# Cross attention: sums of probabilities, their spreading and the value weights' products, each moved behind the value products of their step

## The reference, cut to what matters

```python
kvx = einsum('bsi,oi->bso', cond, w_kv_x)      # cond: 16 x 1500 x 256, kept in float32
kx, vx = split(kvx, 2)                         # 8 groups of 128 each
kx = _ln(kx, kxln_w, kxln_b)
p = softmax(einsum('bsghd,btgd->bghst', qx, kx) / sqrt(128))
xout = einsum('bghst,btgd->bsghd', p, vx)      # 16 heads, 56 queries, 1500 keys
catq = _div_clamp_fp8(cat([core, xout]), proj_smooth)
```

## Time and profile before

| | us |
|---|---|
| median of 3 runs (lowest, highest) | 2561.54 (2557.67, 2563.57) |
| the profiled execution, its own time | 2560.54 |
| its span, first to last instruction | 2558.5 |
| cross attention, from first scores to last `ca` | 1123.8 to 2310.8 |
| TensorE busy over the span | 2341.7 (92%) |
| mean granted clock of TensorE | 0.95 of full |

### The profile page before, as it was taken

The page is one execution under the profiler, slowest core; times in us unless marked ns, Lnnn a source line. Parts: engine busy times, 40 slices in busy tenths (PEclk is TensorE's granted clock), DMA queues, the critical chain, the costliest instruction groups (busy, mean ns, idle before and its releaser), DMA issues. The chain is left out here.

```text
span 2558.5 us, 38343 instructions
## 1 busy us (share of the span) xinstructions
PE 2341.7 (92%) x12603; PEld 2045.3 (80%) x12603; DVE 2019.6 (79%) x3952; ACT 1088.3 (43%) x1849; POOL 919.4 (36%) x640
## 2 busy tenths in 40 slices
PE   7999999999984788859999999999999999986797
PEld 6777777779983666658888888988888888976797
DVE  8999987877757887848888888888888888871487
ACT  1000001108855666614544554455545454554332
POOL 5455100200012344424545544555455444570000
PEclk9999999999996888879999999999999999997899
DMA  9667623517624010042222212222222112106211
GB/s 389 263 266 274 240 99 145 191 66 255 220 98 144 37 44 36 29 135 77 84 74 79 69 46 80 83 80 69 74 83 71 63 57 83 61 4 162 56 55 39
DMA packets 143384, 286.66 MB, mean 112 GB/s; under 512 B 26033, under 2 KB 114178, under 8 KB 139202
## 3 DMA queue, kind: packets, MB, share of 16 engines
q1 hardware_dynamic: 137266, 265.40, 30.0%
q0 software_dynamic: 6032, 20.20, 2.1%
HBM read 203.91 MB, written 81.66 MB: 112 GB/s over the span
## 5 line engine op out<-in xcount | busy, mean ns | idle before, releaser
L1697 POOL TENSOR_TENSOR s_acc<-s_acc,s_sx 125x896 f32<-125x896 f32 x128 | 275.8, 2154 | 261.3 <-DVE s_mxh L1941 114.6
L572 DVE BATCH_NORM_STATS2 s_st<-ps 125x6 f32<-125x128 f32 x1536 | 318.7, 280 | 55.6 <-PE ps L444 49.1
L1896 DVE TENSOR_TENSOR s_sx<-ps,keep_krs 125x896 f32<-125x896 f32 x192 | 208.9, 1088 | 167.3 <-PE ps L1807 164.1
L1761 ACT ACTIVATE s_sx<-s_sx 125x896 f32<-125x896 f32 x192 | 183.2, 954 | 352.8 <-DVE s_sx L1914 352.8
L1858 PE MATMUL ps<-s_p_hi,s_cn_hi 125*128 125x448 f32 x768 | 304.1, 396 | 6.6 <-DVE s_p_lo L1920 6.2
L1920 DVE TENSOR_TENSOR s_p_lo<-s_sx,s_p_hi 125x896 fp32r<-125x896 f32 x192 | 290.7, 1514 | 3.1 <-ACT s_p_hi L1766 3.1
L1807 PE MATMUL ps<-s_qc_hi,s_ct_hi 128*125 128x448 f32 x768 | 288.3, 375 | 1.3 <-DVE s_qc_lo L1879 1.3
L1858 PE MATMUL ps<-s_p_lo,s_cn_hi 125*128 125x448 f32 x768 | 285.1, 371 | 0.0
L1858 PE MATMUL ps<-s_p_hi,s_cn_lo 125*128 125x448 f32 x768 | 285.1, 371 | 0.0
L1807 PE MATMUL ps<-s_qc_lo,s_ct_hi 128*125 128x448 f32 x768 | 282.5, 368 | 0.0
L1807 PE MATMUL ps<-s_qc_hi,s_ct_lo 128*125 128x448 f32 x768 | 282.3, 368 | 0.0
(11 more groups left out here) (378 smaller groups left out, 5646.1 us busy)
## 6 DMA issues: line engine op xcount, KB each, us to landing
l_ahead<-in_ctxt SPq DMA_DIRECT2D x16, 1500.0 KB, 8.6
s_ct_hi<-ct_hi SPq DMA_DIRECT2D x48, 500.0 KB, 4.2
s_ct_lo<-ct_lo SPq DMA_DIRECT2D x48, 500.0 KB, 4.9
s_cn_raw<-in_ctx SPq DMA_DIRECT2D x48, 500.0 KB
l_raw<-in_ctxt SPq DMA_DIRECT2D x15, 1500.0 KB, 10.4
l_raw<-in_w SPq DMA_DIRECT2D x16, 1024.0 KB, 5.4
ct_hi<-l_hi SPq DMA_DIRECT2D x8, 1500.0 KB, 12.1
ct_lo<-l_lo SPq DMA_DIRECT2D x8, 1500.0 KB, 16.3
```

The costliest lines, as they stand in the source:

```text
L572: ins = dve.bn_stats(st[:, G * t + g, :], kx[0:TT, t % NB, g // 4, DH * (g % 4):DH * (g % 4) + DH])
L1697: pool.tensor_tensor(a, a, p[:, PR * w.pt:PR * w.pt + PR, :], ALU.add).then_inc(s["acc_ready"], 1)
L1761: act.activation(p, p, ACT.Exp).then_inc(s["exp_ready"], 1)
L1896: dve.tensor_tensor(by_group(sx[w.h][:, tiles, :]), by_group(sc[st % 2]), krs_b[:, tiles, HG * w.h:HG * w.h + HG].unsqueeze(3).to_broadcas ...
```

## The change

In the cross attention alone, nothing is added or removed; eight edits move work within the steps.

- TensorE: the value products of a step come right after its scores and what belongs to the maxima, ahead of the sums, the spread and the value weights' products.
- ScalarE: in step 3 the copy to `ut` comes first and `rdiag` no longer follows it there but begins step 4; `rsc` begins step 5 and not step 4.
- VectorE: the reciprocal `r4` goes from behind L1896 to the end of step 3; `ca` goes from step 5 to step 0 of the next unit, behind `p_lo`.
- The tail has one more call, for `ca` of the last unit.

```diff
@@ steps_of
             body(B)
+            act(B + 1, 0)
             act(B + 1, 3)
@@ ScalarE
-                    if w.i == 3 and w.two_back:
+                    if w.i == 4 and w.two_back:
                         act.wait_ge(s["r4_ready"], w.u - 1)
...
                         ins.then_inc(s["rdiag_ready"], 1)
...
-                    if w.i == 4 and w.two_back:
+                    if w.i == 5 and w.two_back:
                         act.wait_ge(s["rb_ready"], w.u - 1)
@@ TensorE: this block is moved up, from behind the value weights' products
+                    if w.has_v:
+                        pe.wait_ge(s["lo_ready"], w.v + 1)
+                        if w.vt == 0 and not (static(w.vu) and w.vu < 1):
+                            pe.wait_ge(s["ut_read"], w.vu)
...
+                        for j in range(PR):
+                            t = PR * w.vt + j
...
+                        mm.then_inc(s["pv_ready"], 1)
                     if w.i == 3 and w.two_back:
                         pe.wait_ge(s["acc_ready"], NPR * (w.u - 1))
@@ VectorE
-                    if w.i == NPR - 1 and w.two_back:
-                        dve.wait_ge(s["rb_read"], w.u - 1)
-                        dve.wait_ge(s["v_ready"], w.u - 1)
+                    if w.i == 0 and w.three_back:
+                        dve.wait_ge(s["rb_read"], w.u - 2)
+                        dve.wait_ge(s["v_ready"], w.u - 2)
                         dve.tensor_tensor(ca[:, :], misc[:, 0:QH], rsc[:, :], ALU.mult).then_inc(s["v_read"], 1)
...
+                    if w.i == 3 and w.two_back:
+                        dve.wait_ge(s["sum_ready"], w.u - 1)
...
+                        dve.reciprocal(r4[:, :], sums).then_inc(s["r4_ready"], 1)
```

More of the change, by code:

```diff
@@ L1821, in run @@
                         pe.matmul(mb, ones_r[:, :], diag[:, :, :], start=True, stop=True).then_inc(s["mb_ready"], 1)
+                    if w.has_v:
+                        pe.wait_ge(s["lo_ready"], w.v + 1)
+                        if w.vt == 0 and not (static(w.vu) and w.vu < 1):
+                            pe.wait_ge(s["ut_read"], w.vu)
+                        if w.vh == 0 and PR * w.vt % CHT == 0:
+                            vb = b + (st - V_LAG) // STEPS
+                            pe.wait_ge(s["cn_lo_ready"], NCH * vb + PR * w.vt // CHT + 1)
+                        for j in range(PR):
+                            t = PR * w.vt + j
+                            for k in range(K2):
+                                c = 0
+                                for x, pp in ((cn_hi, (p_hi, p_lo)), (cn_lo, (p_hi,))):
+                                    for y in pp:
+                                        mm = pe.matmul(pv[:, k, :], x[:, t, k * P:k * P + P], y[w.vr][:, j, :],
+                                                       start=(t == 0 and c == 0), stop=(t == NT - 1 and c == 2))
+                                        c += 1
+                        mm.then_inc(s["pv_ready"], 1)
                     if w.i == 3 and w.two_back:
@@ L1844, in run @@
                         mm.then_inc(s["v_ready"], 1)
-                    if w.has_v:
-                        pe.wait_ge(s["lo_ready"], w.v + 1)
-                        if w.vt == 0 and not (static(w.vu) and w.vu < 1):
-                            pe.wait_ge(s["ut_read"], w.vu)
-                        if w.vh == 0 and PR * w.vt % CHT == 0:
-                            vb = b + (st - V_LAG) // STEPS
-                            pe.wait_ge(s["cn_lo_ready"], NCH * vb + PR * w.vt // CHT + 1)
-                        for j in range(PR):
-                            t = PR * w.vt + j
-                            for k in range(K2):
-                                c = 0
-                                for x, pp in ((cn_hi, (p_hi, p_lo)), (cn_lo, (p_hi,))):
-                                    for y in pp:
-                                        mm = pe.matmul(pv[:, k, :], x[:, t, k * P:k * P + P], y[w.vr][:, j, :],
-                                                       start=(t == 0 and c == 0), stop=(t == NT - 1 and c == 2))
-                                        c += 1
-                        mm.then_inc(s["pv_ready"], 1)
                     if w.i == 1 and w.new and w.next:
@@ L1904, in run @@
                         qc_split(w.u + 1, 1 - w.h, 0)
-                    if w.i == 3 and w.two_back:
-                        dve.wait_ge(s["sum_ready"], w.u - 1)
-                        if not (static(b) and w.u < 3):
-                            dve.wait_ge(s["rdiag_ready"], w.u - 2)
-                        dve.reciprocal(r4[:, :], sums).then_inc(s["r4_ready"], 1)
                     if w.has_p:
```

10 lines of the change are left out of this document (6 added, 4 removed).

## The result

The changed kernel took 2526.36 us (median of 4 runs, 2524.0 to 2527.13), the kernel before 2559.88 on the same chip (4 runs, 2557.67 to 2563.57): a ratio of 0.9866, 95% interval 0.9849 to 0.9883. Run twice more, it gave 2526.03 (0.9867, 0.9851 to 0.9884) and 2526.53 (0.987, 0.9848 to 0.9891). Forecast were 2530 and a range of 2522 to 2545. The profiled execution took 2525.84 with a span of 2523.8 us, against 2560.54 and 2558.5.

A forecast was written before the change was run, and what follows sets the result against it. TensorE's queue was taken to bound the kernel, standing still mainly at the sums. Terms 21.2 - 3.5 + 6.3 + 6.4 = 30.4 us off the profiled 2560.5 gave 2530, range 2522 to 2545.

The forecast's parts named there:

- The waits at the sums: Steady units, TensorE: value products first remove waits of 1.18 us in 14 odd and 0.36 in 13 even units, 21.2 us.
- The clock: Four of 14 odd units, steps 3 and 4: slow-clock stretches of 1.57 us each all go, 6.3 us.
- The new wait for `p_lo`: Step 5 of 14 odd units: value products wait 0.25 us for `p_lo` of step 4, 3.5 us back.
- The lower bound of 0: Smallest size of the step 5 `p_lo` wait: GpSimd's chain follows fully and `p_lo` is not blocked.
- the 24.0 of the terms: Steady units: 21.2 us for the sums' waits, minus 3.5 for `p_lo`, plus 6.3 for the clock.
- The tail: After the last scores: GpSimd's chain 3.3 us sooner, sums to spread 3.05 shorter; 6.4 us, at least 3, at most 8.
- The edits priced at nothing: Moved `ut`, reciprocal, `rdiag`, `rsc`, value weights' products and `ca` cost nothing in steady units; `ca` covered by 0.4 us.
- VectorE and GpSimd did not become the pace: Rival, odd units: their chain does not tighten and the 1.18 us wait returns at step 5 or spread; 2543 to 2549, chance 0.12.
- The clock did not stay slow: Rival, odd units: the clock dips stay because thin sums stay; 2536, chance 0.10.
- The collisions: Rival, steps 4 and 5 of odd units: two more blocked `p_lo` per pair of units cost 46 us; 2576, chance 0.05.
- It does not do what it says: Rival, at the sums: a second wait stood just behind `qc_lo`; 2555 to 2561, chance 0.04.
- Odd units of 35.5: Sign, scores to scores: odd units take 35.5 us instead of 36.4; wrong if still 36 or more.

The follow-up runs named there:

- The filler of 0.62 us: The changed kernel with 0.62 us of extra VectorE work ahead of `p_lo` in step 4 of odd units; 2528.46 us, ratio 0.9884.
- the run with the earlier add: The changed kernel, but GpSimd's first add of step 3 no longer waits for that step's running maximum; 2593.76 us, ratio 1.0144.

## Why the prediction was right, and where its terms were off

**The waits at the sums: 21.2 predicted, about 23.5 measured.** This term was right. Odd units without a slow clock went from 36.4 to 35.1, 1.3 and not 1.18; even ones from 35.6 to 35.2, 0.4 and not 0.36. The difference is the sums themselves: they held TensorE 0.80 us behind a wait and hold it 0.72 now (1653.48 - 1652.76). It is 0.80 to 0.83 in the steady units of the other runs in which they wait, too. 27 x 0.08 = 2.2 us that the term had left out.

**The clock: 6.3 predicted, about 8.1 measured.** All four slow stretches (units 5, 11, 19 and 27) went, as taken. A slow odd unit cost 1.5 to 1.6 us, as worked out, and in three of the four cases the even unit behind it another 0.6 to 0.7 (36.2 or 36.3 in place of 35.6), which the two windows of the earlier trace rows end too early to show. That second part is a collision and not the clock. The kernel before in step 1 behind the first slow unit, on TensorE, VectorE and GpSimd:

```profile
1324.86 0.47 PE L1858 MATMUL ps<-s_p_hi,s_cn_hi 125*128 125x448 f32 x1 [0.40 <-DVE s_p_lo L1920]
...
1321.50 3.31 DVE L1920 TENSOR_TENSOR s_p_lo<-s_sx,s_p_hi 125x896 fp32r<-125x896 f32 x1
...
1321.44 2.42 POOL L1705 TENSOR_TENSOR s_cn_lo<-s_cn_raw,s_cn_hi 125x1024 fp32r<-125x1024 f32 x1
```

and in the same step of an even unit that follows no slow one:

```profile
1394.67 1.08 DVE L1920 TENSOR_TENSOR s_p_lo<-s_sx,s_p_hi 125x896 fp32r<-125x896 f32 x1
...
1394.70 3.31 POOL L1705 TENSOR_TENSOR s_cn_lo<-s_cn_raw,s_cn_hi 125x1024 fp32r<-125x1024 f32 x1
```

`p_lo` is 0.06 us behind `cn_lo` in the one and 0.03 ahead in the other, and takes 3.31 or 1.08. It is 3.31 behind three of the four slow units, and TensorE waits for it there.

**The new wait for `p_lo`: 3.5 predicted, none measured.** This is the step that failed. The prediction moved GpSimd's start by the right amount: its first add is released by the running maximum (217.2 us in 27 waits) and starts 25.7 us into the unit where it had started 26.2 into it. But the prediction left VectorE's `p_lo` where it was, and the change moves that further. VectorE's scaling of the scores in step 4 had waited 1.11 us for them, and that wait is gone. `p_lo` starts 27.65 us into the unit and no longer 28.92, and so 0.17 ahead of `cn_lo`. The filler of 0.62 us put the order back, and the wait with it. The lower bound of 0, "`p_lo` not blocked", was what happened. The Trainium skill, SBUF — State Buffer, section "SBUF: two separate sides", gives the shared ports to whichever of the two starts first, for its whole instruction, and has the other blocked. The traces agree on who is held, in both directions: with `cn_lo` first, `p_lo` 2.75 and `cn_lo` 2.41; with `p_lo` first, `p_lo` 1.16 and `cn_lo` 3.25. The prediction used the second half of this and did not ask who would start first after the change.

**Steady part in sum:** 2.3 + 1.8 + 3.5 = 7.6 us better than the 24.0 of the terms, and -32.2 measured leaves 0.6 to rounding. In all the profiled executions differ by 34.7 us where 30.4 were forecast. The forecast gain was 8.2 too small in the steady part; the tail and the later start of the stage took 0.9 and 2.5 of that back.

**The tail: 6.4 predicted, 5.5 measured.** Counted from the first scores of the last unit (2222.49 before, 2193.03 now), GpSimd's first add came at 57.4 before and comes at 54.0: 3.4, against 3.3. From sums to spread it is 3.6 less, against 3.05. Then 1.5 us are given back behind the spread, since the last products run at 1.2 GHz; this the prediction did not have. The 4.64 us that the transposes wait for the moved `ca`, also not foreseen, is mostly covered: the version without it has a tail of 81.2 and 82.8, the changed kernel one of 82.8, 82.7 and 83.0. That the tail is off by only 0.9 is in part luck: one term was 0.5 too small, and a loss of 1.5 was missing.

**The edits priced at nothing.** That was right of all but `ca` in the place it was moved to. Left in their old places beside the rest of the change, the reciprocal and `rdiag` cost about 20 us of the steady part, the value weights' products 16. `ca` was priced at nothing with 0.4 us of cover. VectorE was to begin step 0 up to 0.9 us after its scores end; in even units it begins 1.3 after (1669.60, scores over at 1668.3), the cover is used up, and about 2 us are lost by the traces. `ca` could better have stayed.

**The rivals.** VectorE and GpSimd did not become the pace: odd and even units are equal, at TensorE's. The clock did not stay slow. The collisions did not reach TensorE (they moved from `p_lo` to the running maximum), but the run with the earlier add shows what they can do: 67 us of steady part from one wait less, where the rival had 46. "It does not do what it says" is excluded by the 0.5 that the sums still wait.

**What would show it.** Sums without idle time ahead: yes. A wait for `p_lo` in odd units: no. Clock 1.00: yes. Odd units of 35.5: 35.1. First add released by the maximum: yes. `p_lo` not longer: shorter, 1334 ns. All other stages as they were: yes, up to the spread of the stage's start.

How the 7.5 us of the moves on VectorE and ScalarE divide among them was not separated: taking the reciprocal and `rdiag` back alone costs 20.3, most of it because the moved `ca` is then late, and `rsc` was never taken back alone.

## What to carry to other kernels

When an in-order queue stands at a small block whose input comes late, look for a large block behind it whose input is already there, and try moving the consumers of the small block's result along with it. Left behind, the reciprocal and the diagonal cost 7.5 to 20 us of the steady part here, depending on what else was moved; `ca` cost nothing left behind and about 2 us moved, so each needs its own sum. Look at the late input as well: making `qc_lo` earlier, a move of one instruction on VectorE, gave 23.4 of the 32.2 us by itself. Before pricing a collision of VectorE and GpSimd, work out the start of both sides after the change, since less than a tenth of a microsecond can decide which is held, and ask what is queued behind the one that wins, since that is held next. A cover of less than half a microsecond should be listed as a place that breaks if the engine in front is late for any other reason.
